# A four-layer graph network: first layer in one block, folded projections, earlier tables, edge weights in PSUM, and unread products on TensorE

## The reference

```python
def _L0_gnn_ref(x, edge_index, W, b):
    w = dinv_sqrt[row] * dinv_sqrt[col]
    h = jax.ops.segment_sum(w[:, None] * x[col], row, num_segments=N)
    h = h @ W + b
    return jnp.where(h >= 0, h, LEAKY_ALPHA * h)

def _L1_gnn_ref(h, src, dst, W_lin, b_lin, W_gat, attn_l, attn_r, gat_bias):
    h = h @ W_lin + b_lin
    h_in = h
    feat = (h @ W_gat).reshape(N, NUM_HEADS, OUT_DIM)
    el = jnp.sum(feat * attn_l, axis=-1)
    er = jnp.sum(feat * attn_r, axis=-1)
    e = jax.nn.leaky_relu(el[src] + er[dst], 0.2)
    m = jax.ops.segment_max(e, dst, num_segments=N)
    e = jnp.exp(e - m[dst])
    s = jax.ops.segment_sum(e, dst, num_segments=N)
    msg = feat[src] * (e / s[dst])[:, :, None]
    out = jax.ops.segment_sum(msg, dst, num_segments=N)
    out = jax.nn.leaky_relu(out.reshape(N, NUM_HEADS * OUT_DIM) + gat_bias, 0.01)
    return h_in + out

# _L2_gnn_ref: dot-product attention, then three mean-aggregating layers
def _L3_gnn_ref(h, weight, norm, src, dst, rel_type):
    transformed = jnp.einsum('ni,rio->rno', h, weight)
    msg = transformed[rel_type, src] * norm
    return jax.ops.segment_sum(msg, dst, num_segments=h.shape[0])

x = _layernorm(x + _L0(x)); x = _layernorm(x + _L1(x)); x = _layernorm(x + _L2(x)); x = _layernorm(x + _L3(x))
```

## Time and profile before

| | |
|---|---|
| Time, median of 3 runs | 5126.87 us (5117.08 to 5129.01) |
| The profiled execution, its own time | 5111.43 us |
| Its span | 5109.8 us |
| PE busy | 3956.6 us (77%) |
| DVE busy | 1992.5 us (39%) |
| POOL busy | 1339.3 us (26%) |
| ACT busy | 604.2 us (12%) |
| HBM traffic | 493 MB, 96 GB/s over the span |

### The profile page before, as it was taken

How to read it: one execution, slowest core, us unless ns; L and a number is a source line. 1 busy time by engine, 2 the same in 40 slices (tenths; PEclk the granted TensorE clock), 3 DMA queues, 4 the chain that set the end, 5 groups by cost and what they waited for, 6 DMA issues and landing times. The chain is left out here.

```text
span 5109.8 us, 55063 instructions
## 1 busy us (share of the span) xinstructions
PE 3956.6 (77%) x15645; PEld 2395.3 (47%) x15646; DVE 1992.5 (39%) x4598; ACT 604.2 (12%) x1188; POOL 1339.3 (26%) x947
## 2 busy tenths in 40 slices
PE   4999996996625655647999979999999599655454
PEld 2444444884424433335666654655556344333332
DVE  6988773004537666563322311212112311111113
ACT  0011111222200000001222210000000122100000
POOL 1000000000057765203777730000000000266662
PEclk9999998998656666779999989999999799766665
...
GB/s 45 13 51 51 77 77 132 240 247 77 32 104 118 105 110 89 36 11 67 71 77 74 69 111 135 119 139 121 136 131 108 66 148 142 128 88 90 90 89 56
DMA packets 284806, 494.52 MB, mean 97 GB/s; under 512 B 22297, under 2 KB 207933, under 8 KB 273165
## 3 DMA queue, kind: packets, MB, share of 16 engines
...
## 5 line engine op out<-in xcount | busy, mean ns | idle before, releaser
L1069 POOL DMA_INDIRECT e7got<-rel_d,rel_i x416 | 395.5, 951 | 1633.4 <-SPq L1053 1419.4
L531 PE MATMUL c_counts<-c_hot_s,c_hot_d 128*128 128x512 bf16 (+1 forms) x2912 | 596.8, 361 | 5.6 <-DVE c_hot_d L508 2.7
L1177 POOL DMA_INDIRECT a_got<-feat_d,src_i x416 | 460.2, 1106 | 444.9 <-POOLq L1499 223.6
L761 PE MATMUL s_aggs<-s_blk,h 128*128 128x512 f32 (+1 forms) x1400 | 549.9, 549 | 16.8 <-DMA s_blk<-turned_d 16.8
L1093 PE MATMUL e7sums<-e7got,e7hot 128*128 128x256 f32 x832 | 330.0, 543 | 218.0 <-issue 169.2
L531 PEld LDWEIGHTS c_counts<-c_hot_s,c_hot_d 128*128 128x128 bf16 x2912 | 266.3, 99 | 302.1 <-issue 15.3
L761 PEld LDWEIGHTS s_aggs<-s_blk,h 128*128 128x128 f32 x1400 | 264.4, 191 | 267.6 <-issue 176.3
L1941 PE MATMUL q_prods<-w,q_xt 128*128 128x512 f32 x800 | 353.0, 599 | 13.4 <-ACT q_xt L1959 13.4
L1093 PEld LDWEIGHTS e7sums<-e7got,e7hot 128*128 128x128 f32 x832 | 199.5, 264 | 339.0 <-issue 287.6
L853 DVE TENSOR_SCALAR s_zs<-s_prods,col 128x256 f32<-128x256 f32 x75 | 36.3, 484 | 751.9 <-PE s_prods L787 751.9
L1079 DVE TENSOR_SCALAR e7hot<-iota,dloc,weight 128x128 f32<-128x128 f32 x416 | 119.3, 361 | 516.6 <-PE e7sums L1093 362.1
...
## 6 DMA issues: line engine op xcount, KB each, us to landing
...
```

What stands on the lines that cost most here:

```text
L531: last = pe.matmul(counts[:, b, 0:taken[b]], hot_d[:, u, :], hot_s[:, u, b * 512:b * 512 + taken[b]], start=False, stop=False)
L761: last = pe.matmul(aggs[:, idx % 2, half, 0:w], feats[l][:, a, half * P:(half + 1) * P], blk[:, q % RINGS, a % GA, 0:w], start=a == 0, sto ...
L1069: pool.indirect_dma_start(got[:, j % U, :], None, table, bass.IndirectOffsetOnAxis(ap=index[:, j:j + 1], axis=0)).then_inc(arrived[j % U], 16)
L1177: pool.indirect_dma_start(got[:, n % 2, s, :], None, table, bass.IndirectOffsetOnAxis(ap=k.src_i[:, j:j + 1], axis=0)).then_inc(arrived[n ...
```

## The change

Five things are changed.

`root_layer` takes the place of the load, `inverse_root`, `scale_tiles`, `dense_product` and "p0". The scaled features `r` become the stationary operand and up to 512 columns of `pairs_d` the moving one. The columns are taken in seven chunks (4, 4, 4, 4, 3, 3 and 3 tiles, each 5 loads), and the sum comes out turned, so that the projection multiplies it without transposes; it stands between the groups of the next chunk. Loads and the stores of `turned_d` both go through SP's queue. The root and the scaling run in the same block.

`compose_weights` multiplies W_lin by W_gat and folds the score vectors into further columns, in a block of its own with the loads, and one `project` of 528 columns takes the place of "p1" and "p2".

"e7" has 52 gather buffers and 52 tables in place of 26 and 13.

In `attend` the tile `upto` goes: its values are written to the PSUM tile `turned`. ACT writes the exponentials a second time, to PSUM, and DVE's multiply reads them there.

Also in `attend`, `busy` issues products on TensorE whose result nobody reads: 8 ahead of the wait for `scanned`, 3 ahead of that for `carried`, 10 ahead of that for `topped`, and 3 behind the transposes of the maxima.

```diff
+def root_layer(nc, k, mat_d, turned_d, r, new, col, w, bias, loads):
+    RINGS, LINES = 5, 3
+    GROUPS = T // GA
+    NCH = len(CHUNKED)
...
+            for n, (first, count) in enumerate(CHUNKED):
+                for g in range(GROUPS):
+                    q = n * GROUPS + g
+                    if q >= RINGS:
+                        sp.wait_ge(used, q - RINGS + 1)
+                    sp.dma_start(blk[:, q % RINGS, :, 0:count * P],
+                                 mat_d[g * GA * P:(g + 1) * GA * P, first * P:(first + count) * P].rearrange(
+                                     "(a p) q -> p a q", p=P)).then_inc(loaded[q % RINGS], 16)
+                    if q >= RINGS:
+                        store(q - RINGS)
...
+            def group(n, g):
+                q = n * GROUPS + g
+                count = CHUNKED[n][1]
+                w = count * P
+                if g == 0 and n >= 2:
+                    pe.wait_ge(kept, 2 * (n - 1))
+                pe.wait_ge(loaded[q % RINGS], (q // RINGS) * 16 + 16)
+                for a in range(g * GA, (g + 1) * GA):
+                    m = n * T + a
+                    if m >= 2:
+                        pe.wait_ge(lined, m - 1)
+                    for s in range(count):
+                        last = pe.transpose(flips[:, m % 2, s * P:(s + 1) * P], blk[:, q % RINGS, a % GA, s * P:(s + 1) * P],
+                                            k.ident[:])
+                    last.then_inc(flipped, 1)
+                    if n == 0:
+                        pe.wait_ge(scaled, a + 1)
+                    for half in range(2):
+                        last = pe.matmul(aggs[:, n % 2, half, 0:w], r[:, a, half * P:(half + 1) * P],
+                                         blk[:, q % RINGS, a % GA, 0:w], start=a == 0, stop=a == T - 1)
+                last.then_inc(used, 1)
...
+            def beside(n, g):
+                first, count = CHUNKED[n]
+                if 1 <= g <= count:
+                    multiply(n, first + g - 1)
+            for n in range(NCH):
+                for g in range(GROUPS):
+                    group(n, g)
+                    if n >= 1:
+                        beside(n - 1, g)
...
+                step(dve.scalar_tensor_tensor(z, prods[:, t % 2, 0:D], col[:, t:t + 1], bias[:], ALU.mult, ALU.add))
+                step(dve.scalar_tensor_tensor(z, z, 0.2, z, ALU.mult, ALU.max))
+                dve.tensor_tensor(new[:, t, :], k.X[:, t, :], z, ALU.add).then_inc(finished, 1)
...
-    U, V = 26, 52
+    U, V = 52, 52
-        hot = sb("hot", [P, 13, P])
+        hot = sb("hot", [P, U, P])
...
-                        dve.wait_ge(multiplied, j + U - 4)
-                    dve.tensor_scalar(hot[:, u % 13, :], k.iota[:], cols(k.dloc, j, 1), cols(weight, j, 1),
+                        dve.wait_ge(multiplied, j + 4)
+                    dve.tensor_scalar(hot[:, u, :], k.iota[:], cols(k.dloc, j, 1), cols(weight, j, 1),
...
-                step(dve.tensor_tensor_scan(flat(upto[:]), flat(penx[:, 0, :, :]), v, -BIG, ALU.add, ALU.max))
-                step(dve.tensor_tensor_scan(flat(both[:])[:, ::-1], flat(penx[:, 1, :, :])[:, ::-1], flat(upto[:])[:, ::-1],
+                step(dve.tensor_tensor_scan(v, flat(penx[:, 0, :, :]), v, -BIG, ALU.add, ALU.max))
+                step(dve.tensor_tensor_scan(flat(both[:])[:, ::-1], flat(penx[:, 1, :, :])[:, ::-1], v[:, ::-1],
...
-                    step(dve.tensor_tensor(upto[:], small[0:CS, 4 * CS + d * H:4 * CS + (d + 1) * H].unsqueeze(2).broadcast_to([CS, H, P]),
+                    step(dve.tensor_tensor(v.rearrange("q (h p) -> q h p", h=H), small[0:CS, 4 * CS + d * H:4 * CS + (d + 1) * H].unsqueeze(2).broadcast_to([CS, H, P]),
                                            reach[:, d, :].unsqueeze(1).broadcast_to([CS, H, P]), ALU.add))
-                    step(dve.tensor_tensor(both[:], both[:], upto[:], ALU.max))
+                    step(dve.tensor_tensor(both[:], both[:], v.rearrange("q (h p) -> q h p", h=H), ALU.max))
...
-                dve.wait_ge(weights, n + 1)
+                dve.wait_ge(weights, 2 * n + 1)
...
-                    dve.tensor_tensor(rows, rows, got[:, b, 4 * g:4 * g + 4, D:W].unsqueeze(3).broadcast_to([P, 4, H, HD]),
+                    share = peaks[:, 256 + 4 * g * H:256 + (4 * g + 4) * H].rearrange("p (s h) -> p s h", h=H)
+                    dve.tensor_tensor(rows, rows, share.unsqueeze(3).broadcast_to([P, 4, H, HD]),
...
+            def busy(count):
+                for _ in range(count):
+                    pe.matmul(expand[:, 0, 384:512], k.ident[:], k.ones[:], start=True, stop=True)
             def maximum(n, b, more):
                 if more:
                     spread_scores(n + 1, 0, 2)
+                    busy(8)
...
                     spread_scores(n + 1, 2, 4)
+                    busy(3)
...
                     spread_scores(n + 1, 4, 6)
+                    busy(10)
...
+                    busy(3)
                     spread_scores(n + 1, 6, 8)
...
+                pe.wait_ge(weights, 2 * n + 2)
+                pe.sem_inc(k.passed, 1)
...
+                act.activation(peaks[:, 256:256 + H * CS].rearrange("p (s h) -> p s h", h=H), own[:], ACT.Exp).then_inc(weights, 1)
                 act.activation(got[:, b, :, D:W], own[:], ACT.Exp).then_inc(weights, 1)
...
+def compose_weights(nc, k, wide, gat, bias, al, ar, loads):
...
+        @block.tensor
+        def _(pe):
+            pe.wait_ge(loaded, 16 * len(loads))
+            for m in range(2):
+                for a in range(2):
+                    last = pe.transpose(flips[:, (2 * m + a) * P:(2 * m + a + 1) * P], wide[:, a, m * P:(m + 1) * P], k.ident[:])
+            last.then_inc(flipped, 1)
+            for m in range(2):
+                last = pe.transpose(flips_b[:, m * P:(m + 1) * P], bias[:, m * P:(m + 1) * P], k.ident[:])
+            last.then_inc(flipped, 1)
+            pe.wait_ge(turned, 1)
+            for a in range(2):
+                for m in range(2):
+                    last = pe.matmul(prods[:, a * D:(a + 1) * D], lin_t[:, 2 * m + a, :], gat[:, m, :], start=m == 0, stop=m == 1)
+            last.then_inc(multiplied, 1)
+            pe.wait_ge(turned, 2)
+            for m in range(2):
+                last = pe.matmul(prods_b[:, 0:D], bias_t[:, m, :], gat[:, m, :], start=m == 0, stop=m == 1)
+            last.then_inc(multiplied, 1)
...
+            for n, scores in enumerate((al, ar)):
+                here = slice(2 * D + n * H, 2 * D + (n + 1) * H)
+                if n == 0:
+                    dve.wait_ge(kept, 2)
+                step(dve.tensor_tensor(junk[:, 0:2, :], prods[:].rearrange("p (a n) -> p a n", a=2),
+                                       scores[:].unsqueeze(1).broadcast_to([P, 2, D]), ALU.mult))
+                if n == 0:
+                    dve.wait_ge(kept, 3)
+                step(dve.tensor_tensor(junk[:, 2, :], prods_b[:, 0:D], scores[:], ALU.mult))
+                step(dve.tensor_reduce(wide[:, :, here], junk[:, 0:2, :].rearrange("p a (h f) -> p a h f", h=H), AX.X, ALU.add))
+                step(dve.tensor_reduce(bias[:, here], junk[:, 2, :].rearrange("p (h f) -> p h f", h=H), AX.X, ALU.add))
...
-            load(nc, "l0", [(w[:], halves(L0_gnn_W)), (b[:], spread(L0_gnn_b))])
-            inverse_root(nc, k, col)
-            r = sl("r0", [P, T, D])
-            scale_tiles(nc, r, k.X, col)
-            if debug: debug(nc, 'y', r)
-            agg = sl("agg0", [P, T, D])
-            dense_product(nc, k, "d0", pairs_d, r, agg, col, turned_d)
-            z = sl("z0", [P, D])
-            def epilogue(dve, step, t, p):
-                step(dve.tensor_tensor(z[:], p[:, 0:D], b[:], ALU.add))
-                step(dve.scalar_tensor_tensor(z[:], z[:], 0.2, z[:], ALU.mult, ALU.max))
-                step(dve.tensor_tensor(tile_of(r, t), tile_of(k.X, t), z[:], ALU.add))
-            project(nc, k, "p0", [(agg, None)], w, D, 3, epilogue)
-            normalize(nc, k, "n0", r, k.X)
+            r, agg = sl("r0", [P, T, D]), sl("agg0", [P, T, D])
+            root_layer(nc, k, pairs_d, turned_d, r, agg, col, w, b, [(w[:], halves(L0_gnn_W)), (b[:], spread(L0_gnn_b))])
+            normalize(nc, k, "n0", agg, k.X)
...
-                project(nc, k, "p1", [(k.X, None)], w, D, 1,
-                        lambda dve, step, t, p: step(dve.tensor_tensor(tile_of(h, t), p[:, 0:D], b[:], ALU.add)))
+                compose_weights(nc, k, wide, gat, bias, al, ar,
+                                [(wide[:, :, 0:D], halves(L1_gnn_W_lin)), (gat[:], halves(L1_gnn_W_gat)),
+                                 (bias[:, 0:D], spread(L1_gnn_b_lin)),
+                                 (al[:], spread(L1_gnn_attn_l.rearrange("h f -> (h f)"))),
+                                 (ar[:], spread(L1_gnn_attn_r.rearrange("h f -> (h f)"))),
+                                 (gb[:], spread(L1_gnn_gat_bias))])
                 def epilogue(dve, step, t, p):
```

(9 more changed lines are left out.)

162 lines of the change are left out of this document (126 added, 36 removed).

## The result

The changed kernel takes 5153.69 us in the median of 5 runs (5142.87 to 5156.13), the kernel before 5120.43 (5115.61 to 5129.01). The ratio is 1.0065, 95% interval 1.0043 to 1.0087: slower by 33 us, where 175 us less were forecast. The profiled execution has a span of 5152.5 us.

What follows compares the result with a forecast made beforehand. TensorE was taken to bound the first layer and e7's stream, waits the attention. Start and first layer -51, projections -43, attention -36, e7 -45 gave -175 from 5111.4; with 15.4 for the median, 4952 us, range 4892 to 5022.

Steps and rivals of the forecast that it cites:

- e7: Stage from its first gather to n3's first operation: more tables and gather buffers cut TensorE's waits, -45 us of 638.
- First layer and projections: Start through new projection: earlier first transpose and projection columns between products, -51 us; one folded projection for two, -43 us.
- D, the starved queue: First layer: loads and stores on SP's queue alone limit it, +202 us there, 5154 us in total; chance 0.02.
- behind each wait they cost nothing while the clock is up: Attention: unread products, 0.21 to 0.26 us each at full clock, hide in TensorE's waits for DVE and add nothing.
- writing `upto` to PSUM costs nothing by itself: Attention: moving the scan's result out of SBUF is free in itself and changes only GpSimd's gathers.
- the shorter gathers: Attention: gathers falling from 1106 to 951 ns give POOL 65 us, which goes into its 90.8 us wait for the sum.
- +8 was the bound: Attention's worst case: clock stays down, each chunk pays 0.2 us at the wait and 0.5 before the next scores.
- A: Attention: unread products don't raise the clock, +4 us in place of -36, total 4992 us; chance 0.14.
- "issue": e7: 169.2 + 52.5 us in which TensorE stands, taken as no one's wait and part of the bounding stream.
- The table term: e7: tables up to 48 ahead remove TensorE's wait for tables, 32.8 us, within the stage's -45.
- its far bound (550 us): e7: TensorE follows POOL, whose floor is 550 of the 638 us, a gain of 88 us.
- B: e7 stays at TensorE's own pace of issue, the table wait only renamed: -10 us, total 4987 us; chance 0.13.

## Why the prediction was wrong

**First layer and projections.** Right, in mechanism and within 7 us each: -58 for -51, -48 for -43. The product's group didn't change, the projection's columns went in between, the clock of the new projection came up to 0.98. D, the starved queue, is refuted: loads and stores went through SP's queue at 222 GB/s.

**Attention: the step that failed.** It was the step "behind each wait they cost nothing while the clock is up" together with "writing `upto` to PSUM costs nothing by itself" and the shorter gathers, whose time "goes into that wait". With slow stretches the PSUM copies cost 94 us and the unread products 28 to 45, where +8 was the bound. The products were priced by TensorE's columns, 0.21 to 0.51 us each; in a slow stretch an instruction costs 0.7 us or a multiple, whatever its columns, each product is two plus two weight loads, and three products took 8.1 us. The gain on the other side wasn't there either. The sum's first 24 half products, priced at 5.9 us, take about 10 with and without the products, and without slow stretches the kernel before with the whole set of products takes 4920.4 us against 4922.3. So A (no gain from the clock) was the right rival in kind, and it left out the price.

The PSUM copies are worth -14 us without slow stretches (722 to 708), not the up to 65 that POOL got back. On the gathers the trace agrees with the first half of what the Trainium skill says (SBUF — State Buffer, Who interferes with whom), that a DVE instruction with two SBUF inputs contends with a GpSimd instruction that reads SBUF: the mean gather went from 1106 to 998 ns here, and from 1156 to 1004 in executions without slow stretches. The page's inference that a tensor_tensor doesn't hold up descriptor generation is contradicted by one run. With the weights back in SBUF and the scans still in PSUM the mean is 1071, and the gathers that overlap the multiplication, a tensor_tensor, take 1303 ns on average where they take 1063 with the weights in PSUM. With the scan's result back in SBUF instead it is 1058, and those beside the scans take 1406 ns, against 945. A gather beside no DVE instruction takes 946.

The estimate itself rested on one chunk of 48.9 us that I took as the steady state. The 12 periods from scan to scan had a mean of 56.2 before and have 65.8 after; without slow stretches they have 49.8 (kernel before with unread products) and 48.6 (changed kernel without them). The chunk I priced was one without a slow stretch, and its first 24 half products took 8.1 us where the mean of the 12 was 11.7.

**e7: the second step that failed.** It was to take the 32.8 us named after a table, and TensorE's "issue", 221.7 us, as what they are called. The table term was put at -32.8. With 52 tables there were 48 ready in the median, of 416 products one found none but its own, and still 11.4 us stand under the table's name in the changed kernel, 29.3 in its second trace, and 50.1 without slow stretches. So that row didn't measure a lack of tables; what it did measure is open. "Issue" I took as a fixed pace of its own. It is no property of the loop: the same loop has 14.9 us of it without slow stretches. There TensorE follows POOL, which the prediction had as its far bound (550 us), and e7 takes 534 to 539.

With 52 buffers e7 took 666 to 678 us in six traces with slow stretches, with 26 644.6 in the one that there is. Slow stretches go with trains of gathers, that is gathers that follow each other without a wait. By the count there are some 240 of them in the eight traces; all but three began within a train, and those three within 1 us behind one; half ended 1.3 to 3.5 us after the last gather of the train, and nine in ten no later than 4.4. The first train of e7 takes 55 us with 26 buffers and 94 to 96 with 52, and its slow stretch lasts from 20 to 66 us after the first gather, or from 15 to 18 until 107 to 115: 46 us against 89 to 97. So the loss fits the longer lead, but the run that should have shown it met no slow stretch, and it stays argued. A train alone doesn't make one: without slow stretches the gathers follow each other through all of e7. B came closest (169.2 to 207.5), yet e7 grew.

**The sum.** Of -175 us there were -106 in the two parts that are plain work, and +150 in the two that consist of waits.
What stays open: why an execution has slow stretches or not, what holds up the streams in them, and why the PSUM copies lengthen the periods. Shown is that they come beside trains of gathers, that TensorE's, ACT's and DVE's streams are stopped and GpSimd's isn't, and that they come and go with the execution and not with the kernel: the kernel without unread products took 5103.0 us in one set and 4807.5 in another, and the kernel before 5099 and 4920 at two times on the same chip.

The best version depends on that too. The changed kernel without unread products and with e7's old buffers took 4803.4 us, 2.4% less than the kernel before (0.9756), where there were no slow stretches; with them the changed kernel with the old attention is the best that was run, 5013.3 us (0.9838). In the other kind that attention gives up little: with e7 at 13 buffers the same kernel took 4819.5 us there.
